# One more wait on VectorE: the maximum of the next graph's first heads waits for GpSimd's power of the first norm

## The chip, the cores and the metric

The kernel runs on 1 core of a Trainium2 chip. The metric is the device time of one execution in microseconds. The engines are called by name or as in the profile: PE (TensorE), DVE (VectorE), ACT (ScalarE), POOL (GpSimd), SP (SyncE, which issues the DMAs).

## The reference

128 independent graphs, each with 128 nodes, 512 features and an adjacency matrix `adj` of 128 by 128. Two layers, each behind a norm and a relu:

```python
h = jnp.maximum(_layernorm(x), 0.0)
x = x + L0(h, adj, W, b, a_self, a_neigh)       # attention, 8 heads of 64
h = jnp.maximum(_layernorm(x), 0.0)             # "the first norm's" h below
x = x + L1(h, adj, W1, b1, gamma, beta, W2, b2) # hypergraph, 512 -> 1024 -> 512

# L0
dense = leaky_relu(e_self[..., :, None] + e_neigh[..., None, :], 0.2)
att = softmax(dense - 1e10 * (1 - A)); out = relu(att @ feats + b)
# L1
H = (adj != 0); w = first row of adj
conv(x, W, b) = Dinv * (H @ (Binv * (H.T @ (x @ W.T)))) + b
h = layer_norm(relu(conv(x, W1, b1)), gamma, beta);  return conv(h, W2, b2) + x
```

`_layernorm` is `(x - mean) / sqrt(var + 1e-5)` over the 512 features, without a scale or an offset.

## The kernel before

All is in fp32. Where accuracy asks for it, products are made as three products of split operands (`_hi` and `_lo`; L838, L839, L843 and L832 to L834). Each engine runs a program of its own, written as a function `turn(t)`, and the engines meet only at semaphores. In turn t the five engines work on several graphs at once: on graph t its second layer, on t+1 the end of its attention and the second layer's norm and first product, on t+2 the attention scores, on t+3 the first product, on t+4 and t+5 the first steps of the input. `turns` writes out the first and the last turns and puts the 120 between them into a loop of 4 turns each; there the awaited count of a semaphore stands in a register. The order on each engine is the order of the code in `turn`, written by hand.

What lies around the change, for graph t+1 in turn t. The attention's output is added to `x` (`x1`, L755), and its statistics are taken (L758, L770, all on VectorE). L774 makes `ve1`, the variance plus epsilon, and L775 `nm1`, the negative mean. GpSimd raises `ve1` to -0.5 (L392, `rs`; the power of the title) and multiplies `nm1` by it (L346, `nb`). Then ScalarE makes `h` from `x1`, `rs1` and `nb1` (L517). TensorE multiplies `h` by the graph's matrix `G` into `p_w1b` (L953). ScalarE rounds this to `hg_hi` (L527), VectorE takes the rest `hg_lo` (L802), and the next turn's products of 512 to 1024 features begin.

The attention's scores are two exponentials for each head, `att` and `att_low` (L457, L458), of which VectorE takes the larger (L601, `larger`), in two halves of four heads. The larger of the first half of graph t+2 stands right behind L775 in turn t. That of the second half of graph t+1 stands earlier in the turn, behind L652; it also shows as L601. The result of both is first read by the transposes L897, which wait for both halves of their graph. Behind the first-half maximum VectorE comes to L789 (`z`), which waits for TensorE's second product (L843 on `p_w1a`, `rT_lo`).

In the trace, buffer numbers are left out (`ve`, `rs`, `nm`, `nb`, `h`).

Of the kernel before, what the change touches and what calls it, by code (L numbers as in the profile page):

```python
# [64 lines left out]
def gnn_two_layers(nc, x, xT, adj2, W0T, b0, a_self, a_neigh, W1T, b1, gammaT, betaT, W2T, b2, out):  # L65
    NG, N, D = x.shape
# [14 lines left out]
    with ctx:  # L81
# [3 lines left out]
        def sem(name):  # L85
            return ctx.enter_context(nc.semaphore(name))
# [96 lines left out]
        s_stats1, s_mv1, s_ve1, s_rs1, s_nm1, s_nb1, s_h, s_xh, s_rest = (sem("s_" + n) for n in ("stats1", "mv1", "ve1", "rs1", "nm1", "nb1", "h", "xh", "rest"))  # L183
# [371 lines left out]
        def _(dve):  # L555
# [33 lines left out]
            def centre(m):  # L589

                for c in range(CB):
                    last = nc.vector.scalar_tensor_tensor(
                        piece(3 + m)[:, c, :], piece(3 + m)[:, c, :], gamma_beta[:, 0, m * CB + c:m * CB + c + 1],
                        mean_sb, ALU.mult, ALU.subtract)
                last.then_inc(k_cent, 1)

            def larger(g, half):

                dve.wait_ge(s_exp, g.count(per=2) - 1 + half)
                heads = slice(half * HH, (half + 1) * HH)  # L600
                nc.vector.tensor_tensor(att[:, heads, :], att[:, heads, :], att_low[:, heads, :], ALU.max).then_inc(s_att, 1)  # L601
# [7 lines left out]
            def turn(t):  # L609
# [166 lines left out]
                if t.base == -1:  # L776
                    dve.wait_ge(k_mean_sb, 2)
                    centre(0)
                    centre(1)
                if t.plus(2).within(NG):  # L780
                    larger(t.plus(2), 0)
                g = t
                if g.within(NG):
# [19 lines left out]
                if g.within(NG):  # L803
                    nc.vector.bn_aggr(mv0, st0[:, :]).then_inc(s_mv0, 1)

            turns(dve, turn, NG, {-3: setup_wa})

        @block.tensor
# [201 lines left out]
```

## Time and profile before

| | |
|---|---|
| median of 3 runs | 2591.59 us (2589.86 to 2593.36) |
| the profiled execution's own time | 2593.87 us |
| its span | 2591.9 us |
| mean granted TensorE clock | 0.993 of full speed |
| busy: PE, DVE, POOL, ACT | 98%, 76%, 63%, 55% of the span |
| instructions: PE, DVE, ACT, POOL | 14996, 4640, 3465, 2068 |

Durations in the profile come from one execution, so sums are set against its time and then carried to the median. PEld is TensorE's weight load, which runs ahead of the matmuls. A busy PE is not PE at its peak; idle time of an engine counts only where it is waited for.

### The profile page before, as it was taken

What the parts mean: (1) busy time and instruction counts of PE and PEld (TensorE: products, weight loads), DVE (VectorE), ACT (ScalarE), POOL (GpSimd) and SP (SyncE); (2) the same over time, 40 slices, a digit from 0 to 9 for tenths busy, and PEclk for the clock granted to TensorE, in tenths of its full rate; (3) what the DMA queues carried; (4) which work ended last, traced back from release to release, by engine and by line L of the source; (5) the groups of instructions that cost most, each with busy time, mean ns of one, the idle gap of its engine ahead of it and who ended that gap; (6) DMA issues with size and microseconds to landing.
All of it is one profiled execution on the core that took longest, in us unless ns stands there. A gap on an engine that the chain in (4) does not pass through costs nothing.

```text
span 2591.9 us, 50876 instructions
## 1 busy us (share of the span) xinstructions
PE 2527.3 (98%) x14996; PEld 2195.1 (85%) x14996; DVE 1968.6 (76%) x4640; ACT 1423.3 (55%) x3465; POOL 1630.6 (63%) x2068
## 2 busy tenths in 40 slices
PE   3899999999999999999999999999999999999998
PEld 2788888888888888888888888888888888888886
DVE  5877777777777777777777777777777777777774
ACT  2555555555555555555555555555555555555553
POOL 4666666666666666666666666666666666666663
PEclk8899999999999999999999999999999999999999
DMA  5122222222222222222222222222222222222210
GB/s 183 63 75 80 77 76 80 74 79 77 73 79 74 80 79 74 80 76 77 77 73 79 74 80 79 74 80 79 74 80 72 82 79 71 79 75 80 79 65 26
DMA packets 105480, 201.89 MB, mean 78 GB/s; under 512 B 20080, under 2 KB 36464, under 8 KB 105456
## 3 DMA queue, kind: packets, MB, share of 16 engines
q1 hardware_dynamic: 105456, 201.60, 23.5%
q8 instruction: 11, 0.18, 0.0%
q14 instruction: 13, 0.11, 0.0%
HBM read 167.39 MB, written 34.15 MB: 78 GB/s over the span
## 4 chain that ended last, share of the span: by engine, by line
PE 85%; DVE 8%; issue 3%; POOL 2%; DMA 1%; ACT 1%; SPq 0%; POOLq 0%; DVEq 0%
PE p_w1a L843 12%; PE p_w1a L839 12%; PE p_w1a L838 12%; PE p_att L917 7%; PE p_w1b L953 5%; PE p_w1b L839 5%; PE p_w1b L843 5%; PE p_w1b L838 5%; PE p_att L897 4%; PE p_fa L834 2%; PE p_fa L832 2%; PE p_fa L833 2%; PE p_fb L832 2%; PE p_fb L833 2%; PE p_fb L834 2%
## 5 line engine op out<-in xcount | busy, mean ns | idle before, releaser
L392 POOL TENSOR_TENSOR rs<-ve,halfpow 128x1 f32<-128x1 f32 x128 | 117.8, 921 | 544.8 <-DVE ve L774 544.8
L380 POOL TENSOR_TENSOR u<-u,mask 128x1024 f32<-128x1024 f32 x128 | 306.3, 2393 | 182.0 <-DMA u<-en_rows 182.0
L838 PE MATMUL p_w1a<-W_hi,rT_hi 128*128 128x512 f32 x1024 | 415.5, 406 | 0.0
L457 ACT ACTIVATE att<-u,shifts 128x128 f32<-128x128 f32 x1024 | 400.5, 391 | 18.4 <-DVE shifts L734 10.5
L839 PE MATMUL p_w1a<-W_lo,rT_hi 128*128 128x512 f32 x1024 | 404.1, 395 | 0.0
L458 ACT ACTIVATE att_low<-u,shifts 128x128 f32<-128x128 f32 x1024 | 399.5, 390 | 0.0
L843 PE MATMUL p_w1a<-W_hi,rT_lo 128*128 128x512 f32 x1024 | 280.8, 396 | 0.0
L502 ACT ACTIVATE rT_hi<-p_tb 128x512 fp32r<-128x512 f32 x128 | 76.6, 598 | 333.5 <-PE p_tb L864 333.5
L917 PE MATMUL p_att<-feats,attT 128*128 128x65 f32 x2048 | 242.9, 272 | 2.2 <-ACT attT L492 2.2
L917 PEld LDWEIGHTS p_att<-feats,attT 128*128 128x128 f32 x2048 | 239.6, 192 | 2.7 <-ACT attT L492 2.7
L789 DVE SCALAR_TENSOR_TENSOR raw<-p_w1a,rs,t_bc 128x512 f32<-128x512 f32 x128 | 96.1, 750 | 187.2 <-PE p_w1a L843 187.2
L652 DVE SCALAR_TENSOR_TENSOR raw<-p_w1a,inv,b_bc 128x512 f32<-128x512 f32 x128 | 96.1, 751 | 183.9 <-PE p_w1a L843 183.9
L843 PEld LDWEIGHTS p_w1a<-W_hi,rT_lo 128*128 128x128 f32 x1024 | 192.3, 188 | 46.6
L517 ACT ACTIVATE h<-x,nb,rs 128x512 f32<-128x512 f32 x128 | 104.4, 816 | 230.6 <-POOL nb L346 230.6
L839 PEld LDWEIGHTS p_w1a<-W_lo,rT_hi 128*128 128x128 f32 x1024 | 193.0, 188 | 39.9
L838 PEld LDWEIGHTS p_w1a<-W_hi,rT_hi 128*128 128x128 f32 x1024 | 192.4, 188 | 40.6
L838 PE MATMUL p_w1a<-W_hi,hg_hi 128*128 128x512 f32 x512 | 213.3, 417 | 1.1 <-ACT hg_hi L527 1.1
L411 POOL TENSOR_TENSOR raw<-x,h 128x512 f32<-128x512 f32 x128 | 164.0, 1281 | 64.4 <-issue 63.9
L838 PE MATMUL p_w1b<-W_hi,hg_hi 128*128 128x512 f32 x512 | 203.4, 397 | 0.0
L839 PE MATMUL p_w1b<-W_lo,hg_hi 128*128 128x512 f32 x512 | 203.1, 397 | 0.0
L839 PE MATMUL p_w1a<-W_lo,hg_hi 128*128 128x512 f32 x512 | 202.1, 395 | 0.0
L483 ACT ACTIVATE rT_hi<-p_ta 128x512 fp32r<-128x512 f32 x128 | 76.6, 598 | 220.9 <-PE p_ta L864 220.9
(125 smaller groups left out, 7216.9 us busy)
## 6 DMA issues: line engine op xcount, KB each, us to landing
u<-en_rows SPq DMA_DIRECT2D x130, 576.0 KB, 3.6
x_in<-in_x SPq DMA_DIRECT2D x128, 256.0 KB, 2.6
xT_in<-in_xT SPq DMA_DIRECT2D x128, 256.0 KB, 3.2
out<-raw SPq DMA_DIRECT2D x128, 256.0 KB, 2.0
adj_in<-in_adj SPq DMA_DIRECT2D x128, 128.0 KB, 2.5
en_rows<-eT SPq DMA_DIRECT2D x520, 1.1 KB
raw<-in_W1T SPq DMA_DIRECT2D x2, 1024.0 KB, 8.1
raw<-in_W2T SPq DMA_DIRECT2D x2, 1024.0 KB, 9.7
```

Source lines behind the costliest of these rows:

```text
L380: nc.gpsimd.tensor_tensor(u[:, g.slot(2), 0:HEADS, :], u[:, g.slot(2), 0:HEADS, :], mask[:, :].unsqueeze(1).broadcast_to([P, HEADS, N]), A ...
L392: nc.gpsimd.tensor_tensor(rs1[:, :], ve1[:, :], halfpow[:, :], ALU.pow).then_inc(s_rs1, 1)
L411: nc.gpsimd.tensor_tensor(rest[:, s, :], x1[:, s, :], h[:, s, :], ALU.add).then_inc(s_xh, 1)
L457: nc.scalar.activation(att[:, i, :], u[:, g.slot(2), i, :], ACT.Exp, bias=shifts[:, 0, i:i + 1])
L458: last = nc.scalar.activation(att_low[:, i, :], u[:, g.slot(2), i, :], ACT.Exp, bias=shifts[:, 1, i:i + 1], scale=SLOPE)
L517: nc.scalar.activation(h[:, g.slot(2), :], x1[:, g.slot(2), :], ACT.Relu, bias=nb1[:, :], scale=rs1[:, :]).then_inc(s_h, 1)
L832: mm(dst, hi, w_hi, start=first, stop=False)
L838: mm(dst, hi, w_hi, start=first, stop=False)
L839: mm(dst, hi, w_lo, start=False, stop=False)
L843: return mm(dst, lo, w_hi, start=False, stop=final)
L917: last = mm(p_o[:, i // HH, i % HH, :], attT[:, i, :], feats[:, g.slot(2), i, :], start=True, stop=True)
L953: last = mm(p_w1b[:, c * P:(c + 1) * P], h[:, g.slot(2), c * P:(c + 1) * P], G[:, g.slot(4), 0:N], start=True, stop=True)
```

## The change

On VectorE, the maximum of the first half of graph t+2 now waits until the power of graph t+1 (`s_rs1`, raised by GpSimd's L392) is done.

```diff
--- before.py
+++ after.py
@@ -778,6 +778,8 @@
                     centre(0)
                     centre(1)
                 if t.plus(2).within(NG):
+                    if t.plus(1).within(NG):
+                        dve.wait_ge(s_rs1, t.plus(1).count())
                     larger(t.plus(2), 0)
                 g = t
                 if g.within(NG):
```

No instruction with work moves on any engine. VectorE's listing in the loop, before and then after, from `ve1` to `z`; the brackets name the semaphores that are waited for, and a REGISTER_ALU computes the count that the next wait compares with:

```order
L774 TENSOR_SCALAR ve<-mv 128x1 [waits s_nb1,s_mv1]
L775 TENSOR_SCALAR nm<-mv 128x1
L599 REGISTER_ALU
L601 TENSOR_TENSOR att<-att,att_low 128x512 [waits s_exp]
L789 SCALAR_TENSOR_TENSOR raw<-p_w1a,rs,t_bc 128x512 [waits s_z_lo,s_rs2,s_w2]
```

```order
L774 TENSOR_SCALAR ve<-mv 128x1 [waits s_nb1,s_mv1]
L775 TENSOR_SCALAR nm<-mv 128x1
L599 REGISTER_ALU [waits s_rs1]
L601 TENSOR_TENSOR att<-att,att_low 128x512 [waits s_exp]
L791 SCALAR_TENSOR_TENSOR raw<-p_w1a,rs,t_bc 128x512 [waits s_z_lo,s_rs2,s_w2]
```

The wait is on the register instruction ahead of the maximum; lines behind it count two more. GpSimd's listing at the same place is the same in both kernels:

```order
L392 TENSOR_TENSOR rs<-ve,halfpow 128x1 [waits s_ve1,s_h]
L346 TENSOR_TENSOR nb<-nm,rs 128x1 [waits s_rs1,s_nm1]
L400 TENSOR_TENSOR beT<-inc,inv 128x128 [waits s_G,s_inv]
L402 COPY beT<-adj_in 128x1
L411 TENSOR_TENSOR raw<-x,h 128x512 [waits s_x1,s_h,s_y_sb]
```

`nb` waits there for the same semaphore `s_rs1`. In the turns that are written out VectorE has no register instruction there, and the maximum itself waits for `s_exp` and `s_rs1`.

## Rows read from the trace of the kernel before

**Rows 1.** The page, busy time, share of the span and instructions of each engine.

```profile
PE 2527.3 (98%) x14996; PEld 2195.1 (85%) x14996; DVE 1968.6 (76%) x4640; ACT 1423.3 (55%) x3465; POOL 1630.6 (63%) x2068
```

**Rows 2.** Waits of PEld: whom for, us in total, times, longest us.

```profile
PEld p_w1b L953 <- ACT h L517: 16.9, 40, 3.8
```

**Rows 3.** Timeline of one turn: start us, us, engine, line, operation [idle before <-releaser].

```profile
1215.25 0.68 DVE L601 TENSOR_TENSOR att<-att,att_low 128x512 f32<-128x512 f32 x1
...
1215.42 0.92 POOL L392 TENSOR_TENSOR rs<-ve,halfpow 128x1 f32<-128x1 f32 x1 [4.22 <-DVE ve L774]
...
1216.48 0.19 POOL L346 TENSOR_TENSOR nb<-nm,rs 128x1 f32<-128x1 f32 x1
...
1216.71 0.81 ACT L517 ACTIVATE h<-x,nb,rs 128x512 f32<-128x512 f32 x1 [2.15 <-POOL nb L346]
...
1216.94 0.19 PEld L834 LDWEIGHTS p_fa<-W_hi,h 128*128 128x128 f32 x1
...
1217.57 0.97 PEld L953 LDWEIGHTS p_w1b<-G,h 128*128 128x128 f32 x8 [0.45 <-ACT h L517]
```

**Rows 4.** Timeline of PEld one turn earlier.

```profile
1197.50 0.19 PEld L834 LDWEIGHTS p_fa<-W_hi,h 128*128 128x128 f32 x1
1197.63 0.31 PEld L953 LDWEIGHTS p_w1b<-G,h 128*128 128x128 f32 x2
```

**Rows 5.** Timeline of PEld, L953 where it first and last waits in the steady turns.

```profile
120.48 0.63 PEld L953 LDWEIGHTS p_w1b<-G,h 128*128 128x128 f32 x5 [0.38 <-ACT h L517]
...
2549.35 0.74 PEld L953 LDWEIGHTS p_w1b<-G,h 128*128 128x128 f32 x6 [0.66 <-ACT h L517]
```

**Rows 6.** Waits of DVE: whom for, us in total, times, longest us.

```profile
DVE raw L789 <- PE p_w1a L843: 187.2, 128, 4.3
...
DVE hg_lo L802 <- ACT hg_hi L527: 102.6, 127, 1.3
```

**Rows 7.** Timeline of POOL and ACT in the last graph, which has no next maximum.

```profile
2566.05 0.55 POOL L392 TENSOR_TENSOR rs<-ve,halfpow 128x1 f32<-128x1 f32 x1 [4.41 <-DVE ve L774]
2566.75 0.19 POOL L346 TENSOR_TENSOR nb<-nm,rs 128x1 f32<-128x1 f32 x1
...
2566.97 0.82 ACT L517 ACTIVATE h<-x,nb,rs 128x512 f32<-128x512 f32 x1 [3.50 <-POOL nb L346]
```

**Rows 8.** Groups by tile and line: duration ns min/median/max, first and last start.

```profile
L392 POOL TENSOR_TENSOR rs<-ve,halfpow x128: 549/922/1047, 66.8 to 2566.1; 128x1 f32<-128x1 f32 x128
...
L338 POOL TENSOR_TENSOR ve<-e_blk,eps x128: 185/635/640, 4.8 to 2497.9; 128x1 f32<-128x1 f32 x128
L338 POOL TENSOR_TENSOR ve<-mv,eps x128: 191/191/192, 91.8 to 2579.3; 128x1 f32<-128x1 f32 x128
```

**Rows 9.** Timeline at two waits of DVE: on POOL, and on ACT in the loop.

```profile
44.30 2.34 POOL L380 TENSOR_TENSOR u<-u,mask 128x1024 f32<-128x1024 f32 x1 [4.77 <-DMA u<-en_rows]
46.68 1.22 DVE L725 TENSOR_REDUCE neg_max<-u 128x8 f32<-128x1024 f32 x1 [4.82 <-POOL u L380]
...
1218.77 0.60 ACT L527 ACTIVATE hg_hi<-p_w1b 128x512 fp32r<-128x512 f32 x1 [1.25 <-PE p_w1b L953]
1219.50 0.69 DVE L802 TENSOR_TENSOR hg_lo<-p_w1b,hg_hi 128x512 fp32r<-128x512 f32 x1 [1.14 <-ACT hg_hi L527]
```

**Rows 10.** Timeline of POOL and DVE at two near ties of L367 and L601.

```profile
263.48 0.95 POOL L367 TENSOR_TENSOR mask<-mask,absent 128x128 f32<-128x128 f32 x1
263.49 0.68 DVE L601 TENSOR_TENSOR att<-att,att_low 128x512 f32<-128x512 f32 x1
264.09 0.89 DVE L660 SCALAR_TENSOR_TENSOR h<-xc,h 128x512 fp32r<-128x512 f32 x1
264.39 0.64 POOL L338 TENSOR_TENSOR ve<-e_blk,eps 128x1 f32<-128x1 f32 x1
...
575.91 0.40 POOL L367 TENSOR_TENSOR mask<-mask,absent 128x128 f32<-128x128 f32 x1
575.93 0.92 DVE L601 TENSOR_TENSOR att<-att,att_low 128x512 f32<-128x512 f32 x1
```

## The prediction

> **What bounds the kernel now.** I read the page first: PE is busy for 98% of the span and DVE for 76% [rows 1]. Then I read who PE's weight loads wait for. Behind the start-up, the wait that comes back is the one of the first-norm products `p_w1b` (L953) for `h`, which ScalarE makes [rows 2]. The view counts 40 such waits with 16.9 us; these are only the turns in which the queue ran fully dry. So I went through the timeline turn by turn, in the pattern of [rows 3, 4]. Where `h` is early, L953's first load starts 0.13 us after the load of L834 (1197.50 to 1197.63 in [rows 4]). In [rows 3] it starts 0.63 us after it (1216.94 to 1217.57), so TensorE lost 0.50 us there. From the first such turn to the last [rows 5] I find a loss in 102 of 124 turns, 21.1 us in all and 0.17 us a turn in the mean. In the other 22 `h` is early by up to 0.13 us. The distance from one L953 to the next is 19.42 us plus this loss, with a scatter of 0.01 us: [rows 3, 4] show it as 1217.57 - 1197.63 = 19.94 = 19.44 + 0.50. So TensorE sets the pace, and the chain up to `h` adds to it in most turns. The reader is to see that this is a kernel that is 98% busy and yet pays, nearly one for one, for a delay of `h`.
>
> The loss comes around again, since VectorE's next turn hangs on the same products: ScalarE's rounding of `p_w1b` lets L802 go, for which VectorE waits in 127 turns [rows 6], and behind L802 lie the attention scores, their round trip through memory, the masks and the next norm. A delay of L953 moves both TensorE and the next `h`, so delays add and are not taken back.
>
> **The change, step by step.** One wait is added on VectorE, none is removed, no instruction is moved. Let T be the start of GpSimd's power `rs` (L392).
>
> Before: the maximum (L601, 128x512, two inputs in SBUF) starts 0.17 us ahead of T and ends at T+0.51 (1215.25 + 0.68 = 1215.93, T = 1215.42). The power takes 0.92, `nb` starts at T+1.06, and `h` at T+1.29 [rows 3]. In the last graph there is no maximum of a next graph: there the power takes 0.55, `nb` starts at T+0.70 and `h` at T+0.92 [rows 7]. The power's range over all graphs says the same, 549 least and 922 in the middle [rows 8]. So the maximum holds the power back by 0.37 us, and this is what the wait takes away. Would nothing else happen, `h` would come 0.37 us earlier.
>
> But the maximum is only put off, and what stands behind the power on GpSimd is `nb` (L346), which reads SBUF too, and which `h` waits for. So the question is who is first after the power has ended at T+0.55:
> - `nb` waits for the power's own semaphore and starts 0.14 us after its end (1216.48 against 1216.34 in [rows 3], 0.15 in [rows 7]): T+0.70.
> - VectorE's plain wait on GpSimd costs 0.04 us (46.68 against 44.30 + 2.34, [rows 9]). In the loop the awaited value stands in a register, and a register instruction lies between the wait and the maximum, as the listing of the change shows. The nearest case is L802, also with one: 1219.50 against 1218.77 + 0.60, so 0.13 us [rows 9]. That gives T+0.68 in the loop (120 turns), T+0.59 in the turns written out.
>
> So the maximum starts 0.02 us ahead of `nb`. Near ties of this kind are in the trace, between the other maximum (also L601) and GpSimd's mask L367 [rows 10]. At 263.48 GpSimd starts 0.01 us *before* VectorE and still is the one held: 0.95 us, and VectorE takes its normal 0.68. At 575.91 GpSimd is 0.02 us ahead and wins: 0.40, and VectorE takes 0.92. With GpSimd behind by 0.02 us, VectorE should win by 0.03 us or more over this border.
>
> What a held `nb` costs: an operation of the same size, L338 on 128x1, takes 0.19 us alone [rows 8] and 0.64 when it starts inside VectorE's L660; it then ends 0.05 us after it (264.39 + 0.64 = 265.03 against 264.09 + 0.89 = 264.98, [rows 10]). So `nb` ends at T + 0.68 + 0.68 + 0.05 = T+1.41, and `h` starts 0.04 later (1216.71 against 1216.67 in [rows 3]), at T+1.45: **0.15 to 0.16 us later than now**, although the power itself is faster. In the written-out turns it is T+0.59+0.68+0.05+0.04 = T+1.36, 0.07 later.
>
> The Trainium skill, page "SBUF — State Buffer", section "Who interferes with whom", says that a VectorE instruction with two SBUF inputs contends with a GpSimd instruction that reads SBUF, and that whoever issues first has the port for the whole instruction while the other fully blocks. By that rule the wait moves the contention from the power to `nb`; [rows 10] agree on the holding, and add that "first" has a border of some 0.02 us. [...]
>
> The sum: shift every turn's `h` by 0.155 us against its 124 margins. The 102 turns that lose already take it all, 15.8 us; the 22 others, early by 0 to 0.13, take the remainder, 1.9 us. Less 0.4 us for some 5 written-out turns: +17.3 us. The profiled execution has 2593.87 us (span 2591.9), so 2611.2; it lies 2.28 us above the median of 2591.59, so I forecast **2609 us** (+0.67%).
>
> Costed at nothing: VectorE's own delay. Behind the maximum stands L789, which waits for TensorE's L843 in all 128 turns, 187.2 us or 1.46 us each [rows 6]; the maximum moves back by 0.85 us (T-0.17 to T+0.68), which leaves 0.6. If that cover were gone, the excess would go onto `z`, not needed by TensorE for a further few us. The maximum's own reader is the transposes of the next turn. `beT` and L402 follow `nb` on GpSimd, later by 0.15 us, and their product is TensorE's last of the turn; the next GpSimd step, L411, waits for `h` in any case. DMA issues stand on a queue of their own and move only with the turn.
>
> **The rivals.**
> - *`nb` is first.* If VectorE starts 0.04 us or more later than I take it, for instance since an instruction on an idle engine asks for the port later than one that follows another (as L601 in [rows 10] does), `nb` gets through: `h` at T+0.92, 0.37 early. The loss of each turn falls by up to 0.37; over the 124 margins that is 18.9 of the 21.1 us. 2591.6 - 18.9 = 2573. For it: the margin is 0.03 us only, out of starts rounded to 0.01. Against it: both waits are very regular, and the tie at 263.48 went to VectorE from a worse place. Chance 0.17.
> - *Mixed.* Starts scatter over the border, some turns win 0.37 and some lose 0.16; about one win to one loss leaves 2588 to 2596. Chance 0.07. That the wait does nothing at all I exclude: the power ends after the maximum's present start in every graph.
> - *Held longer.* `nb` pays its whole 0.19 us [rows 8] after VectorE's end, not 0.05. Then `h` is 0.155 + 0.14 = 0.30 us late and the margins give 35 us: 2626. Against it: L338 pays 0.05 in every turn but a few (635 ns in the middle, 640 at most, [rows 8]). Chance 0.03.
> - Main case, held as computed: chance 0.73. Its own range is 2603 to 2616: `h` late by 0.12 us gives +13, by 0.21 gives +24.
>
> **How the numbers follow.** A measurement of this kernel tells some 0.2% (5 us) from no change. Slower: 0.73 + 0.03 = 0.76. Faster: 0.17. Same: 0.07. The main case and the mixed one together hold 0.80, so the range goes from 2588 to 2617 and leaves out the win of `nb` and the longer hold.
>
> **What the profile after would show.** Right: L392 at 0.55 us, L346 grown from 0.19 to some 0.7 us and ending 0.05 us after L601, which starts 0.13 us after the power's end; `h` at T+1.45; L953's first load waiting for `h` in more turns, about 38 us of loss in all; the power's start still 0.15 us behind `ve`. Wrong: L346 still 0.19 us and L601 stretched to about 0.75 us (from T+0.68 to `nb`'s end plus 0.54); then PEld's waits on `h` nearly vanish and the time falls to 2573. If L346 is held but the time stays, delays of `h` don't add up as I claim, and some other wait in the round trip had slack.

## The result, and the profile after

The changed kernel takes 2607.23 us (median of 6 runs, 2604.62 to 2611.41), the kernel before 2589.52 us beside it (6 runs, 2587.65 to 2593.36). The ratio is 1.0064, with a 95% interval of 1.0052 to 1.0076: slower by 0.64%, or about 17 us. The profiled execution took 2611.41 us; the page gives its span and TensorE's share, one point down from [rows 1]:

```profile
span 2609.4 us, 50883 instructions
...
PE 2536.2 (97%) x14996; PEld 2196.6 (84%) x14996; DVE 1981.8 (76%) x4640; ACT 1427.4 (55%) x3465; POOL 1648.6 (63%) x2068
```

One turn's timeline, which answers to [rows 3] (start us, us, engine, line, operation, idle before and its releaser; lines behind the added wait count two more, so L834 is L836 and L953 is L955):

```profile
1223.47 0.55 POOL L392 TENSOR_TENSOR rs<-ve,halfpow 128x1 f32<-128x1 f32 x1 [4.22 <-DVE ve L774]
...
1224.15 0.69 DVE L601 TENSOR_TENSOR att<-att,att_low 128x512 f32<-128x512 f32 x1 [0.75 <-POOL rs L392]
...
1224.17 0.72 POOL L346 TENSOR_TENSOR nb<-nm,rs 128x1 f32<-128x1 f32 x1
...
1224.92 0.81 ACT L517 ACTIVATE h<-x,nb,rs 128x512 f32<-128x512 f32 x1 [2.24 <-POOL nb L346]
...
1225.05 0.19 PEld L836 LDWEIGHTS p_fa<-W_hi,h 128*128 128x128 f32 x1
...
1225.79 0.97 PEld L955 LDWEIGHTS p_w1b<-G,h 128*128 128x128 f32 x8 [0.55 <-ACT h L517]
```

With T = 1223.47 the power is down to 0.55 us. The maximum begins at T+0.68, `nb` at T+0.70, and `nb` now lasts 0.72 us: it ends 0.05 us after the maximum (1224.89 against 1224.84). `h` begins at T+1.45, where it was T+1.29. TensorE's loads come 0.74 us apart (1225.05 to 1225.79) where they are 0.13 us apart without a loss.

The groups by line say that this is so in nearly every turn (duration ns min/median/max): `nb` is held in 126 of 128 graphs, and in the first and the last, where no maximum stands there, it takes 0.19 us. Against [rows 8] the power has lost 0.37 us and `nb` has gained 0.53:

```profile
L392 POOL TENSOR_TENSOR rs<-ve,halfpow x128: 548/549/553, 66.2 to 2583.6; 128x1 f32<-128x1 f32 x128
L346 POOL TENSOR_TENSOR nb<-nm,rs x128: 191/720/723, 66.9 to 2584.3; 128x1 f32<-128x1 f32 x128
```

The waits of PEld and of DVE (us in total, times, longest us), which answer to [rows 2] and [rows 6]:

```profile
PEld p_w1b L955 <- ACT h L517: 37.6, 80, 3.6
```

```profile
DVE hg_lo L804 <- ACT hg_hi L527: 122.5, 127, 1.7
DVE att L601 <- POOL rs L392: 94.6, 126, 0.8
DVE raw L791 <- PE p_w1a L845: 77.9, 121, 4.3
```

TensorE's queue runs dry for `h` in 80 turns, where it was 40. Read turn by turn as in the prediction, the loss at this place is 40.8 us over 124 turns where it was 21.1, in 123 of them where it was in 102, and without it a turn still takes 19.42 us. VectorE's wait for the power, 94.6 us, lies in time that it spent waiting for L845 (187.2 us before, 77.9 now). Run 1 below, in which the maximum comes later still, shows that it costs nothing.

### The profile page after: what moved, and what is told of

It reads as the page before. It is cut to its first block, busy times and chain, and to the rows that moved or that the text cites. A ratio compares the mean times of both kernels' runs of the same rounds, so it can differ in the third digit from the quotient of the medians.

```text
span 2609.4 us, 50883 instructions
## 1 busy us (share of the span) xinstructions
PE 2536.2 (97%) x14996; PEld 2196.6 (84%) x14996; DVE 1981.8 (76%) x4640; ACT 1427.4 (55%) x3465; POOL 1648.6 (63%) x2068
## 4 chain that ended last, share of the span: by engine, by line
PE 65%; DVE 21%; issue 6%; POOL 4%; ACT 2%; DMA 1%; SPq 0%; POOLq 0%; DVEq 0%
PE p_w1a L845 9%; PE p_w1a L840 9%; PE p_w1a L841 9%; PE p_w1b L955 5%; PE p_w1b L845 5%; PE p_w1b L841 5%; PE p_w1b L840 5%; PE p_att L919 4%; DVE neg_max L725 3%; ACT h L517 2%; PE p_att L899 2%; POOL nb L346 2%; DVE st L758 2%; DVE rT_lo L697 2%; DVE rT_lo L749 2%
## 5 line engine op out<-in xcount | busy, mean ns | idle before, releaser
L380 POOL TENSOR_TENSOR u<-u,mask 128x1024 f32<-128x1024 f32 x128 | 306.4, 2394 | 183.6 <-DMA u<-en_rows 183.6
L392 POOL TENSOR_TENSOR rs<-ve,halfpow 128x1 f32<-128x1 f32 x128 | 70.3, 550 | 542.2 <-DVE ve L774 542.2
L845 PE MATMUL p_w1a<-W_hi,rT_lo 128*128 128x512 f32 x1024 | 280.7, 396 | 0.0
L601 DVE TENSOR_TENSOR att<-att,att_low 128x512 f32<-128x512 f32 x256 | 177.8, 695 | 98.4 <-POOL rs L392 94.6
L845 PEld LDWEIGHTS p_w1a<-W_hi,rT_lo 128*128 128x128 f32 x1024 | 192.4, 188 | 46.6
L411 POOL TENSOR_TENSOR raw<-x,h 128x512 f32<-128x512 f32 x128 | 163.6, 1278 | 65.5 <-issue 64.2
```

What stands on the lines that cost most here:

```text
L380: nc.gpsimd.tensor_tensor(u[:, g.slot(2), 0:HEADS, :], u[:, g.slot(2), 0:HEADS, :], mask[:, :].unsqueeze(1).broadcast_to([P, HEADS, N]), A ...
L411: nc.gpsimd.tensor_tensor(rest[:, s, :], x1[:, s, :], h[:, s, :], ALU.add).then_inc(s_xh, 1)
L845: return mm(dst, lo, w_hi, start=False, stop=final)
```

## The experiments

All ratios are to the kernel before on the same chip, with 95% intervals. Three chips took part: runs 1, 2, 6, 8 and the first of 7 stand on one, runs 3, 9, 10 and 11 on a second, runs 4, 5 and the second of 7 on a third. There the kernel before took 2599 to 2605 us and not 2590; run 9 looks at that. The changed kernel itself was not measured beside these runs; run 2, in which the maximum and `nb` start and end as in it, stands in for it. `pad` is a spare tile whose declaration is left out of the code shown, as is that of its semaphore `s_pad`. "Loss" is the sum at the first-norm product over 124 turns, read in each trace as in the prediction. T is always the start of the power. The theory: the maximum and a GpSimd step that meet cannot run side by side, so what counts is which of the steps the maximum holds. The main rival: the added wait puts VectorE's work off, and that costs.

**1. Wait for `nb`, not for the power.** The edit, against the changed kernel:

```diff
-                        dve.wait_ge(s_rs1, t.plus(1).count())
+                        dve.wait_ge(s_nb1, t.plus(1).count())
```

> The maximum waits for nb (L346) in place of the power, so that both GpSimd steps of the norm are free of it. My theory (the wait on the power only moved the hold from the power to nb): power 0.55 us, nb 0.19 us, h at T+0.92 instead of T+1.29 before; the loss at L953 falls from 21.1 to about 2 us, so 18.9 us less than before: ratio to before 0.993. The maximum starts at about T+1.02 and may itself be held by beT (L400) to an end at about T+1.78. Rival (the added wait costs because VectorE's maximum is put off, and z and hg_lo with it): the maximum starts 0.35 us later still than in the changed kernel, so this is slower than it, ratio 1.008 or more.

Measured: 0.9904 (0.9889 to 0.9919), 2574.22 us. Timeline of one turn:

```profile
1205.35 0.55 POOL L392 TENSOR_TENSOR rs<-ve,halfpow 128x1 f32<-128x1 f32 x1 [4.22 <-DVE ve L774]
1206.04 0.19 POOL L346 TENSOR_TENSOR nb<-nm,rs 128x1 f32<-128x1 f32 x1
...
1206.27 0.81 ACT L517 ACTIVATE h<-x,nb,rs 128x512 f32<-128x512 f32 x1 [1.38 <-POOL nb L346]
...
1206.35 0.78 DVE L601 TENSOR_TENSOR att<-att,att_low 128x512 f32<-128x512 f32 x1 [1.09 <-POOL nb L346]
...
1207.27 0.19 PEld L836 LDWEIGHTS p_fa<-W_hi,h 128*128 128x128 f32 x1
1207.40 0.98 PEld L955 LDWEIGHTS p_w1b<-G,h 128*128 128x128 f32 x8
```

`h` begins at T+0.92 and L955 follows L836 in 0.13 us, without a loss; over the run 2.2 us of loss are left. The maximum begins at T+1.00, later than in the changed kernel, and the kernel is faster than both. The rival that the late maximum costs falls here. The maximum's short hold behind `beT` came as expected: 0.78 us, done by T+1.78.

**2 and 3. Memsets to put the maximum behind `nb`.** One memset of 128x1 between wait and maximum, then two.

```diff
                         dve.wait_ge(s_rs1, t.plus(1).count())
+                        nc.vector.memset(pad[:, 0:1], 0.0)
+                        nc.vector.memset(pad[:, 1:2], 0.0)   # the second in run 3 only
```

> The changed kernel, with a memset of 128x1 on a spare tile between the wait on the power and the maximum, so that the maximum starts some 0.1 us later and nb is ahead of it. My theory (whoever is first after the power): nb wins, takes 0.19 us, h at T+0.92, and the maximum is stretched, ending 0.54 us after nb; ratio to before 0.993, though VectorE has more work and a later maximum than in the changed kernel. Rival (the put-off maximum costs by itself): slower than the changed kernel's 1.006. Should nb still be held, the border of who is first lies elsewhere than at a start ahead by 0.02 us: ratio about 1.010.

> The changed kernel with two memsets of 128x1 between the wait and the maximum. With one memset the maximum still began at T+0.68, since the register instruction was done beside the memset, and nb stayed held; the second memset costs 0.07 us more, so the maximum begins at T+0.75, behind nb's T+0.69. My theory (who is first after the power): nb now takes 0.19 us, h comes at T+0.92, the maximum is stretched to about 0.7 to 0.8 us; the time falls from 1.006 of before to 0.990 to 0.993, for 0.07 us more of work and delay on VectorE. Rival (the put-off maximum itself costs): 1.006 or more.

Measured: 1.0060 (1.0046 to 1.0074) and 1.0058 (1.0045 to 1.0070), both as the changed kernel. Timeline with two memsets:

```profile
1206.64 0.06 DVE L784 MEMSET pad<- 128x1 f32 x1 [0.70 <-POOL rs L393]
1206.64 0.06 DVE L785 MEMSET pad<- 128x1 f32 x1
1206.70 0.69 DVE L602 TENSOR_TENSOR att<-att,att_low 128x512 f32<-128x512 f32 x1
```

T is 1206.02 in this turn. The memsets did not put the maximum off: it still begins at T+0.68, so `nb` was still held, 0.73 us. The expectations failed on how to shift it, and the figure of 1.010 that run 2 had for a held `nb` missed as well. The runs tell the theories no further apart.

**4 and 5. Wider memsets,** 128x128 and 128x32, in the same place.

```diff
                         dve.wait_ge(s_rs1, t.plus(1).count())
+                        nc.vector.memset(pad[:, 0:128], 0.0)   # 0:32 in run 5
```

> The changed kernel with one memset of 128x128 between the wait and the maximum. Memsets of 128x1, one or two, did not move the maximum from T+0.68, as the register instruction takes that time anyway. At 0.96 columns a ns at most, 128 columns should add 0.07 to 0.13 us, so the maximum begins near T+0.75 to T+0.8, well behind nb's T+0.69. My theory (who is first after the power decides): nb 0.19 us, h at T+0.92, maximum stretched, ratio 0.990, against 1.006 for the changed kernel, for more work on VectorE. Rival (the put-off maximum costs by itself): 1.006 or more.

> The same with a memset of 128x32, which should put the maximum at about T+0.70 to T+0.72, 0.01 to 0.03 us behind nb's start: the border of who is first, which two near ties of the trace before put at GpSimd ahead by 0.01 to 0.02 us. By these rows nb wins where it is ahead by 0.02 us or more. Either all turns are of one kind (ratio 0.990 or 1.006) or some of each (between), and the trace says at which distance.

Measured: 1.0071 (1.0058 to 1.0085) and 1.0071 (1.0057 to 1.0085). `nb` is held in 126 of 128 graphs in both. The starts were missed again: T+0.72 with 128x128, where T+0.75 to T+0.8 was expected, and with 128x32 T+0.68 as before, still 0.01 us ahead of `nb`, in the turns of the loop. Timeline with 128x128:

```profile
1187.98 0.55 POOL L393 TENSOR_TENSOR rs<-ve,halfpow 128x1 f32<-128x1 f32 x1 [4.22 <-DVE ve L775]
...
1188.62 0.17 DVE L784 MEMSET pad<- 128x128 f32 x1 [0.72 <-POOL rs L393]
...
1188.67 0.73 POOL L347 TENSOR_TENSOR nb<-nm,rs 128x1 f32<-128x1 f32 x1
...
1188.70 0.65 DVE L602 TENSOR_TENSOR att<-att,att_low 128x512 f32<-128x512 f32 x1
```

With 128x128 the maximum's start in the profile is 0.03 us *behind* that of `nb`, and `nb` is held all the same. But the maximum is 0.04 us shorter, and its end is at T+1.37, the same to 0.01 us as with 128x32 and with no memset. So the order of two starts in the profile does not tell who holds whom. One rival stays open: the memset, which runs from 0.05 us ahead of `nb`'s start to 0.12 us behind it, could have held `nb` first. No run has it there without the maximum.

**6. A memset that the maximum waits for.**

```diff
                         dve.wait_ge(s_rs1, t.plus(1).count())
+                        nc.vector.memset(pad[:, 0:1], 0.0).then_inc(s_pad, 1)
+                        dve.wait_ge(s_pad, t.plus(1).count())
```

> The changed kernel with one memset of 128x1 between the wait and the maximum, and the maximum waits for the memset's own semaphore. In the four forms without that wait the maximum ended at T+1.37 in any case and nb was held, so they did not put it off. The memset ends near T+0.67; with 0.13 us for the wait and the register instruction the maximum begins at T+0.80, 0.1 us behind nb. My theory (who is first after the power): nb 0.19 us, h at T+0.92, the maximum is stretched and ends later than in the changed kernel by some 0.1 us or more, and still the ratio falls from 1.006 to 0.990. Rival (the late maximum costs by itself): 1.006 or more. If nb is still held, GpSimd asks for the port over 0.1 us after its start in the profile.

Measured: 0.9911 (0.9894 to 0.9928), 2578.16 us. Timeline:

```profile
1206.68 0.55 POOL L394 TENSOR_TENSOR rs<-ve,halfpow 128x1 f32<-128x1 f32 x1 [4.22 <-DVE ve L776]
...
1207.30 0.06 DVE L785 MEMSET pad<- 128x1 f32 x1 [0.70 <-POOL rs L394]
...
1207.37 0.19 POOL L348 TENSOR_TENSOR nb<-nm,rs 128x1 f32<-128x1 f32 x1
1207.48 0.69 DVE L603 TENSOR_TENSOR att<-att,att_low 128x512 f32<-128x512 f32 x1
1207.51 0.91 POOL L402 TENSOR_TENSOR beT<-inc,inv 128x128 f32<-128x128 f32 x1
1207.60 0.81 ACT L519 ACTIVATE h<-x,nb,rs 128x512 f32<-128x512 f32 x1 [1.68 <-POOL nb L348]
```

This is the run that decides it. The wait on the power is the same as in the changed kernel and VectorE has more to do, but the maximum begins 0.12 us later (T+0.80). `nb` takes 0.19 us, and it is `beT` that is held, 0.91 where it takes 0.40 us; nothing on the way to `h` waits for `beT`. The time goes from 0.6% above the kernel before (run 2, on the same chip) to 0.9% below it. That the maximum would be stretched was wrong: it takes 0.69 us.

The turns that are written out show how close the meeting is. In five of them the maximum starts less than 0.02 us behind `nb`, nearer than in run 4, and `nb` is free:

```profile
97.53 0.19 POOL L348 TENSOR_TENSOR nb<-nm,rs 128x1 f32<-128x1 f32 x1
97.54 0.72 DVE L603 TENSOR_TENSOR att<-att,att_low 128x512 f32<-128x512 f32 x1
...
97.67 0.85 POOL L402 TENSOR_TENSOR beT<-inc,inv 128x128 f32<-128x128 f32 x1
```

This fits the border of the near ties in [rows 10]. Run 4, 0.03 us behind and holding, does not; there a memset runs right ahead of the maximum, and here the maximum has waited for it.

**7. One input in place of two,** at the old place and in the changed kernel. Both leave out the maximum of the first half, so their output is another.

```diff
-                    larger(t.plus(2), 0)
+                    dve.wait_ge(s_exp, t.plus(2).count(per=2) - 1)
+                    nc.vector.reduce_max(pad[:, :], att[:, 0:HH, :], X).then_inc(s_att, 1)
```

> The kernel before, with a maximum over 128x512 of att alone (one input, a reduction into a spare tile) at the place of the maximum of att and att_low; the first four heads' larger is left out, so the output is another. It lasts about as long, 0.6 to 0.7 us, and starts at the same point, ahead of the power. My theory (two inputs in SBUF hold GpSimd): the power takes 0.55 us beside it, h at T+0.92, ratio 0.993. Rival (any VectorE work of that length beside GpSimd's power slows it): the power stays at 0.92 us and the ratio at 1.000.

> The changed kernel, wait included, with a maximum over att alone (128x512, one input) in place of that of att and att_low; the first half's larger is left out, so the output is another. The wait, the late start (T+0.68) and the length (0.68 us) stay, only the second input goes. My theory: nb is not held, h at T+0.92, ratio 0.990. Rival (the wait or the late work on VectorE costs, whatever it reads): 1.006.

Measured: 0.9917 (0.9904 to 0.9931) and 0.9900 (0.9885 to 0.9915). The first has the power at 549 ns in the middle beside a VectorE operation of 0.68 us that begins where the maximum did. In the second, the changed kernel's wait stays:

```profile
1208.72 0.55 POOL L393 TENSOR_TENSOR rs<-ve,halfpow 128x1 f32<-128x1 f32 x1 [4.22 <-DVE ve L775]
...
1209.39 0.69 DVE L785 TENSOR_REDUCE pad<-att 128x4 f32<-128x512 f32 x1 [0.76 <-POOL rs L393]
1209.41 0.19 POOL L347 TENSOR_TENSOR nb<-nm,rs 128x1 f32<-128x1 f32 x1
```

It begins at T+0.67 and runs 0.69 us beside `nb`, which is free. So it is neither the wait nor VectorE's work as such. But two things differ from the maximum: the second input is gone, and the output is 128x4 and not 128x512. The kernel before tells them apart. L802 of [rows 9] writes 128x512 to SBUF with one input in SBUF and one in PSUM, and it runs inside GpSimd's L415:

```profile
1219.01 1.29 POOL L415 TENSOR_TENSOR raw<-raw,b_bc 128x512 f32<-128x512 f32 x1
```

In 127 turns in which they overlap, L802 takes 0.69 us and L415 1.28 to 1.30 us; beside the maximum, in run 10, L415 takes 1.62. The wide output holds nobody, so it is the second input in SBUF. The Trainium skill, page "SBUF — State Buffer", section "Who interferes with whom", states it so: a VectorE instruction with at most one SBUF input, outside the two-port modes, does not contend with GpSimd, and one with two does where GpSimd reads SBUF. These traces agree.

**8. A known delay of `h`, by one more GpSimd link,** in the kernel before.

```diff
+                    pool.wait_ge(s_rs1, g.count())
+                    nc.gpsimd.tensor_tensor(pad[:, 0:1], rs1[:, :], eps[:, :], ALU.add).then_inc(s_pad, 1)
-                    shift(g, nm1, rs1, nb1, s_nm1, s_rs1, s_nb1)
+                    shift(g, nm1, rs1, nb1, s_nm1, s_pad, s_nb1)
```

> The kernel before, with one more GpSimd operation of 128x1 in the chain between the power and nb (nb waits for it; its result is not used). It delays h by 0.27 to 0.33 us without any change to VectorE or to who holds whom. My theory (a delay of h adds turn by turn over the margins): 32 to 39 us more than before, ratio 1.012 to 1.015. Rival (part of a delay of h is taken back by slack in the scores' round trip through memory, and the changed kernel's loss has another cause): clearly less than 25 us, ratio under 1.010.

Measured: 1.0119 (1.0104 to 1.0135), 32 us over the kernel before.

```profile
1210.68 0.92 POOL L394 TENSOR_TENSOR rs<-ve,halfpow 128x1 f32<-128x1 f32 x1 [4.22 <-DVE ve L778]
1211.68 0.19 POOL L396 TENSOR_TENSOR pad<-rs,eps 128x1 f32<-128x1 f32 x1
1212.02 0.19 POOL L348 TENSOR_TENSOR nb<-nm,rs 128x1 f32<-128x1 f32 x1
```

`nb` starts 0.42 us after the power's end instead of 0.14, in the mean 0.27 us later over the turns. The margins of the kernel before, shifted by 0.27, give 32 us. Not all of the measured 32 us is the late `h`: in this trace the turn without its loss takes 19.44 us, 0.02 more than in the kernel before, which makes some 2.5 us. The loss is 56.6 us; what the kernel before loses on this chip was not profiled. The rest, near 30 us, says that a delay of `h` is paid turn by turn, with little or no slack in the round trip.

**9. The kernel before once more, profiled on the chip of runs 3, 10 and 11.**

> The kernel before, unchanged, for its profile on the chip of these runs. Before was 2589.5 us where it was compared with the changed kernel and 2599.0 us beside the first four experiments. My reading (TensorE needs 19.42 us a turn on any chip, and the losses at L953 make the rest) expects 19.42 us a turn again once the losses are taken off, and their sum near 21 us if the time is 2590, near 30 us if it is 2599.

Measured (one run): 2602.65 us. A turn without its loss takes 19.42 us again, and the loss is 30.6 us in 106 of 124 turns. TensorE's pace is the same; the loss is 9.5 us larger than in the first profile, and the execution 8.8 us longer (2602.65 against 2593.87). The two traces show where it comes from. Waits of POOL for the scores' rows that come back from memory, the first profile and then this one:

```profile
POOL u L380 <- DMA u<-en_rows: 182.0, 127, 6.0
```

```profile
POOL u L380 <- DMA u<-en_rows: 193.0, 127, 6.6
```

The transfer `u<-en_rows` takes 3.61 us in the mean from issue to landing there and 3.70 us here. From the start of L802 to that of L380 it is 7.57 and 7.65 us, from L380 to the power 7.93 and 7.92. So the loop is longer by the transfer alone, by 0.08 to 0.09 us a turn. Why the transfer takes longer is open.

Not every edit leaves TensorE's own turn alone: without its loss it is 19.44 us in runs 1 and 11 and 19.46 in runs 6 and 7, up to 5 us over a run. The cause was not looked for, and differences of 0.2% between these runs say nothing.

**10. The maximum behind `z`,** with no wait added.

```diff
-                if t.plus(2).within(NG):
-                    larger(t.plus(2), 0)
...
                                                    ALU.mult, ALU.add).then_inc(s_z, 1)
+                if t.plus(2).within(NG):
+                    larger(t.plus(2), 0)
```

> The kernel before with the maximum moved behind z (L789), with no added wait. Power and nb are free (0.55 and 0.19 us, h at T+0.92), but the maximum now meets GpSimd's x + h (L411, 1.28 us, which reads SBUF) and can be held until that ends, so that hg_lo (L802), for which the scores of the next turn wait on VectorE, starts up to 0.4 us later. My theory expects the gain of h to be given back there in part: ratio 0.994 to 1.001, and in any case more than with the wait on nb (0.990). If VectorE's idle time before hg_lo hides it all, 0.990.

Measured: 1.0025 (1.0016 to 1.0034), a little above my range.

```profile
1204.01 1.63 DVE L601 TENSOR_TENSOR att<-att,att_low 128x512 f32<-128x512 f32 x1
1205.57 0.68 DVE L795 BATCH_NORM_STATS2 st<-x_in 128x6 f32<-128x512 f32 x1
1206.28 0.69 DVE L802 TENSOR_TENSOR hg_lo<-p_w1b,hg_hi 128x512 fp32r<-128x512 f32 x1
```

`h` is at T+0.92 here as well, but the maximum meets GpSimd's L411 (from 1203.82, 1.27 us) and is the one held, 1.63 us. `hg_lo` then starts 0.74 us after `hg_hi` is there (1205.54), where it is 0.13 in [rows 9], and with it the scores of the next turn; it is late by more than 0.2 us in some 90 turns. The loss is 35.5 us, against 30.6 in run 9 on the same chip: the gain is given back at the other end of the same loop. The maximum also holds GpSimd's L415 here, from whose output ScalarE makes `z_hi`; what each of the two is worth was not told apart.

**11. A short maximum at the old place,** 128x4 in place of 128x512. The rest of the first half is left out, so the output is another.

```diff
-                    larger(t.plus(2), 0)
+                    dve.wait_ge(s_exp, t.plus(2).count(per=2) - 1)
+                    nc.vector.tensor_tensor(att[:, 0:HH, 0:1], att[:, 0:HH, 0:1], att_low[:, 0:HH, 0:1], ALU.max).then_inc(s_att, 1)
```

> The kernel before with the maximum at its old place, but over one column of each of the four heads (128x4 in place of 128x512); the rest of the first half's maximum is left out, so the output is another. It still has two inputs in SBUF, but ends before the power needs the port. This is the floor of what any place of the maximum can bring: power 0.55 us, h at T+0.92, ratio 0.990 to 0.993, as with the wait on nb. If VectorE's freed 0.6 us a turn brings something of its own, the ratio is lower than with the wait on nb.

Measured: 0.9899 (0.9885 to 0.9914), with 3.3 us of loss. It is the floor, and the wait on `nb` (0.9904) cannot be told from it. VectorE's freed time brings nothing that shows.

The version to keep is the wait on `nb`: 0.9904, with all of the work done.

## Why the prediction was right

Forecast 2609 us, measured 2607.23: the direction and the size, by the mechanism that was forecast.

- *What bounds the kernel.* A turn costs 19.42 us and the loss at L953. This held in both kernels. Run 8, a known delay of `h` by itself, supports the price: 0.27 us late gives 32 us by the margins, and 32 us were measured, of which some 2.5 belong to a longer turn of TensorE.
- *The power is freed.* Forecast 0.92 to 0.55 us; measured 549 ns in the middle and 553 at most.
- *Who is first.* Forecast: maximum at T+0.68, `nb` at T+0.70, and `nb` held; measured the same. The direction hung on this near tie, and here some luck was in it: in the written-out turns of run 6 the maximum starts at T+0.71 and not at T+0.68, and `nb` is free, which is the opposite outcome. The border read from the near ties fits the changed kernel and run 6. It does not fit run 4, where the maximum holds `nb` from 0.03 us behind, with a memset ahead of it; so the border cannot be relied on.
- *What the hold costs.* Forecast: `nb` ends 0.05 us after the maximum and `h` comes at T+1.45; both measured.
- *The sum.* Forecast +17.3 us; the profiles have +17.5 (2611.41 against 2593.87), the medians +17.7. That it fits to 0.2 us is luck. The loss itself grew by 19.7 us, and the stretch up to the first of these L953, which the sum leaves alone, was 2.1 us shorter (118.39 against 120.48 in [rows 5]). The 2.4 us of loss beyond the forecast fit a term that the sum did not have: from L802 to L380, with the transfer in between, it is 0.02 us a turn longer in this profile than in the one before.
- *The main case's own range.* Its lower end of 2603 does not follow from the +13 us beside it, which give 2605. Nothing else rests on it.
- *VectorE's own delay at nothing.* Its wait of 94.6 us came out of its wait for TensorE's L845, as costed, and run 1 with a later maximum still is faster. Its wait ahead of `hg_lo` grew by the delay of `h`.
- *The rival in which `nb` is first* was wrong for this kernel and right in what it makes of `h` and of the time: runs 1 and 6 are that case. The stretched maximum that was to go with it did not show in run 6; `beT` was held in its place. I gave the rival 2573 us, from a kernel before of 2591.6, or 0.993. Runs 1 and 6 measured 0.990 and 0.991, on chips where the kernel before has more loss to give back: by the margins of run 9's trace, an `h` 0.37 us earlier is worth 26 us, and run 11 on the same chip gained 26.

## What to carry to other kernels

If an operation of one engine holds that of another, a wait moves the meeting to the next operation behind; ask what that is and who waits for it. Here the same wait, put one semaphore further on, gave 1.0% instead of costing 0.6%, with all of the work done; on the chip of the first result, with its smaller loss, an estimate from the margins is 0.7%. On this kernel, whose TensorE is 97% busy, a chain that comes late in most turns is still paid nearly in full; count the margins turn by turn before taking busy time for a cover.

## What was unexpected of the hardware

The order of two starts in the profile does not settle which operation holds the other. The maximum of 128x512 started 0.03 us behind `nb` and `nb` was held (run 4, with a memset running ahead of the maximum); it started less than 0.02 us behind `nb` and `nb` was free (run 6, turns written out). The other maximum started 0.01 us behind the mask L367 and held it, and 0.02 us behind it and was held ([rows 10]). In the loop, memsets of up to 128x128 ahead of the maximum moved its start by at most 0.05 us and its end, near T+1.37, by 0.01 us; a semaphore wait between them moved it to T+0.80.
